# Weight rounding and norm scaling on ScalarE in a four-layer kernel: what moves, engine by engine

## What is computed

```
def _layernorm(x, axis=-1, eps=1e-05):
    m = jnp.mean(x, axis=axis, keepdims=True)
    v = jnp.var(x, axis=axis, keepdims=True)
    return (x - m) / jnp.sqrt(v + eps)
...
        # layer 1's attention: 16 heads of 8 features, 77 keys
        scores = jnp.einsum('bhqd,bhkd->bhqk', q, k) / math.sqrt(D_K)
        scores = jnp.where(m, min_value, scores)
        attn = jax.nn.softmax(scores, axis=-1)
        attn = jnp.where(m, 0.0, attn)
        x = jnp.einsum('bhqk,bhkd->bhqd', attn, v)
...
        # layer 2's feed-forward
        gate = fp4_linear(x, w_gate)
        y = fp4_linear(x, w_up)
        h = jax.nn.silu(gate) * y
        return fp4_linear(h, w_down)
...
        # layer 3's mixture; layers 0 and 1 have mixtures of 8 experts, top 2, of their own form
        h = jax.nn.relu(jnp.einsum('td,edh->eth', xf, w1) + b1[:, None, :])
        y = jnp.einsum('eth,ehd->etd', h, w2) + b2[:, None, :]
        out = jnp.einsum('etd,te->td', y, gf)
...
    x = x + jnp.tanh(g_xattn[0]) * _L0_xattn_ref(_layernorm(x, axis=-1), ctx_1024, ctx_1024, L0_xattn_Wu, L0_xattn_Wv)
    # and so on: one attention and one feed-forward part per layer, four layers
```

## Time and profile before

| quantity | value |
|---|---|
| median of 3 runs | 809.17 us (815.39, 809.17, 808.51) |
| profiled execution, its own time | 815.81 us |
| its span | 814.1 us |
| mean granted clock of TensorE | 0.886 |
| PE busy | 727.3 us (89%) |
| DVE busy | 546.1 us (67%) |
| ACT busy | 371.1 us (46%) |
| POOL busy | 208.1 us (26%) |

### The profile page before, as it was taken

The page is one execution under the profiler, slowest core; times in us unless marked ns, Lnnn a source line. Parts: engine busy times, 40 slices in busy tenths (PEclk is TensorE's granted clock), DMA queues, the critical chain, the costliest instruction groups (busy, mean ns, idle before and its releaser), DMA issues.

```text
span 814.1 us, 10005 instructions
## 1 busy us (share of the span) xinstructions
PE 727.3 (89%) x3459; PEld 572.7 (70%) x3459; DVE 546.1 (67%) x1226; ACT 371.1 (46%) x663; POOL 208.1 (26%) x193
## 2 busy tenths in 40 slices
PE   4989999999999798987999988994659999799997
PEld 2789977888966575865767766773446888577775
DVE  5686769544367767358575765597894554678996
ACT  3365444122235745636338374531213443386773
POOL 5141025320014123114342512035002320213532
PEclk9699999555589999999999989997688999789999
DMA  5120020100000200020202020011000000011000
GB/s 129 40 83 1 1 66 15 65 0 1 0 1 14 65 14 27 0 65 0 79 13 66 18 62 0 1 42 52 0 1 0 2 1 1 4 47 28 1 1 26
DMA packets 27362, 20.97 MB, mean 26 GB/s; under 512 B 5410, under 2 KB 22572, under 8 KB 27312
## 3 DMA queue, kind: packets, MB, share of 16 engines
q1 hardware_dynamic: 26591, 20.29, 8.4%
q10 hardware_dynamic: 720, 0.04, 0.1%
HBM read 19.80 MB, written 0.52 MB: 25 GB/s over the span
## 4 chain that ended last, share of the span: by engine, by line
PE 69%; DVE 18%; issue 4%; ACT 4%; POOL 3%; DMA 1%; ACTq 0%; DVEq 0%; POOLq 0%
PE PS L1433 60%; PE PS L1654 4%; DVE H2l L1124 2%; POOL WL L622 2%; PE PS L1539 2%; ACT H1h L796 1%; PE PS L1590 1%; DVE XN L951 1%; DVE SN L1079 1%; DVE WH L977 1%; PE PS L1454 1%; ACT G L794 1%; DMA GW<-in_L_gate_T 1%; POOL RSTD L632 1%; DVE H1l L1124 1%
## 5 line engine op out<-in xcount | busy, mean ns | idle before, releaser
L622 POOL TENSOR_TENSOR WL<-RAW,WH 128x512 fp32r<-128x512 f32 (+2 forms) x76 | 93.7, 1248 | 166.3 <-DVE WH L977 142.3
L1124 DVE TENSOR_TENSOR H2l<-G,H2h 128x512 fp32r<-128x512 f32 x104 | 84.0, 822 | 62.0 <-ACT H2h L796 61.0
L1124 DVE TENSOR_TENSOR H1l<-G,H1h 128x512 fp32r<-128x512 f32 x80 | 64.6, 814 | 29.5 <-ACT H1h L796 28.6
L1433 PEld LDWEIGHTS PS<-V,ATT 77*128 77x128 f32 x512 | 82.3, 243 | 1.0 <-issue 0.6
L1433 PE MATMUL PS<-V,ATT 77*128 77x9 f32 x512 | 78.7, 282 | 0.0
L813 ACT ACTIVATE ATT<-ATT 128x308 f32<-128x308 f32 x64 | 29.4, 459 | 103.0 <-DVE ATT L1225 102.7
L1217 DVE TENSOR_REDUCE MX<-PS 128x4 f32<-128x308 f32 x64 | 30.5, 477 | 66.9 <-PE PS L1433 66.9
L615 POOL TENSOR_TENSOR RSTD<-VE,MHALF 128x4 f32<-128x4 f32 x18 | 19.3, 1070 | 212.1 <-DVE VE L941 212.1
L1433 PE MATMUL PS<-H1h,WH 128*128 128x512 f32 x146 | 62.1, 425 | 8.0 <-DVE H1l L1124 8.0
L794 ACT ACTIVATE G<-PS,UB 128x512 f32<-128x512 f32 x64 | 44.8, 699 | 40.7 <-PE PS L1433 36.4
L1433 PE MATMUL PS<-XTh,WH 128*128 128x512 f32 x128 | 55.5, 434 | 8.5 <-POOL WL L622 5.3
(11 more groups left out here) (246 smaller groups left out, 1680.3 us busy)
## 6 DMA issues: line engine op xcount, KB each, us to landing
RAW<-in_L_ffn_spec_W SPq DMA_DIRECT2D x4, 1024.0 KB, 5.6
RAW<-in_L_ffn_w SPq DMA_DIRECT2D x16, 256.0 KB, 3.1
RAW<-in_L_ffn_up_W SPq DMA_DIRECT2D x8, 256.0 KB, 2.8
RAW<-in_L_ffn_down_W SPq DMA_DIRECT2D x8, 256.0 KB, 3.3
RAW<-in_L_ffn_spec1a_W SPq DMA_DIRECT2D x2, 512.0 KB, 4.0
RAW<-in_L_ffn_spec1b_W SPq DMA_DIRECT2D x2, 512.0 KB, 5.1
RAW<-in_L_ffn_wg SPq DMA_DIRECT2D x4, 176.0 KB, 2.7
RAW<-in_L_ffn_wu SPq DMA_DIRECT2D x4, 176.0 KB, 2.8
```

The lines of the kernel that those rows point to most:

```text
L622: g.tensor_tensor(lo, RAW[0:r["rows"], r["raw"] + s["c0"]:r["raw"] + s["c1"]], hi.bitcast(fp32), ALU.subtract).then_inc(lo_done, 1)
L1124: v.tensor_tensor(lo, full, hi.bitcast(fp32), ALU.subtract).then_inc(split_done, 1)
L1433: return t_.matmul(o, l, r, start=start, stop=stop)
```

## The change

- `scaled` moves from DVE to ACT everywhere, as `Identity(rstd · x + nmr)` (L734). For this POOL makes NMR = −mean · rstd behind each rstd (L618), DVE makes −mean (NM), and the third and later rstd wait for the scaling of the norm-step two before.
- `high_part` moves to ACT everywhere (L718): for layer 0's first strips, for the six strips of BEFORE[1] (groups 11 to 16 of layer 1's attention), for all strips of mixtures 1 and 3, and for the four strips of BEFORE[3], which leave layer 2 and stand in groups 2 to 5 of layer 3's attention.
- In layer 1 the bias rows are copied on ACT (groups 4, 5, 7 and 9) and subtracted on POOL (L688).
- The attention's weighting in layer 1 is done in PSUM: one `scalar_tensor_tensor` in place of a small scaling and a product into a buffer, then the sum into X.
- norm 4's first half ends in DVE's `stream_plus_norm(0)` at step 8 instead of 10.

The core of the diff:

```
@@ POOL rstd
-                    g.tensor_tensor(RSTD[:, c], VE[:, c], MHALF[:, c], ALU.pow).then_inc(rstd_ready, 1)
+                    if k >= 2:
+                        pool.wait_ge(xn_ready, TH * (k - 1))
+                    step(g.tensor_tensor(RSTD[:, c], VE[:, c], MHALF[:, c], ALU.pow))
+                    g.tensor_tensor(NMR[:, c], NM[:, c], RSTD[:, c], ALU.mult).then_inc(rstd_ready, 1)
@@ POOL, order
-            head_keys(1, CT, range(2, TH + 1))
+            head_keys(1, CT, range(2, 5))
+            for k in range(4):
+                pool.wait_ge(row_high, k + 1)
...
+                g.tensor_tensor(ROWr[32:33, c], ROW[32:33, c], ROWr[32:33, c].bitcast(fp32),
+                                ALU.subtract).then_inc(row_ready, 1)
+            pool.wait_ge(row_ready, 4)
             prepare(1)
...
-            rstd(10, 11)
-            prepare(3)
-            rstd(12, 13)
+            rstd(10, 11, 12, 13)
             pool.wait_ge(k3_ready, 2)
             head_keys(3, K3T, range(2))
             rstd(14, 15)
-            head_keys(3, K3T, range(2, B))
+            for b in range(2, B):
+                for s in BEFORE[3][3 * b - 6:3 * b - 3]:
+                    low_part(s)
+                head_keys(3, K3T, range(b, b + 1))
@@ ACT
+            def scaled(n, h, src, dst):
+                act.wait_ge(rstd_ready, NORM_STEP[n, h] + 1)
+                for t in range(TH * h, TH * h + TH):
+                    s.activation(dst[:, t, :], src[:, t, :], ACT.Identity, scale=RSTD[:, t:t + 1],
+                                 bias=NMR[:, t:t + 1]).then_inc(xn_ready, 1)
@@ ACT attention
+                    if first and 2 <= i < 2 + len(BEFORE[3]):
+                        high_part(BEFORE[3][i - 2])
+                    if not first and i == 6:
+                        scaled(2, 1, X, XN)
+                    if not first and i == TH * NG + WEIGH_LAG - 2 + 4:
+                        scaled(3, 0, X, XN)
+                    if not first and i == TH * NG + WEIGH_LAG - 2 + 9:
+                        scaled(4, 0, XN, XM)
+                    if not first and i in (4, 5, 7, 9):
+                        bias_row((4, 5, 7, 9).index(i))
...
+                    if not first and 11 <= i < 11 + len(BEFORE[1]):
+                        high_part(BEFORE[1][i - 11])
@@ DVE weighted, layer 1
-                        now(v.tensor_scalar(RC2[:, :], RC[:, :], ANY[:, t:t + 1], None, ALU.mult))
-                        rc = RC2
-                        dst = TMP
+                        now(v.scalar_tensor_tensor(o[:, :, 0:DK], o[:, :, 0:DK], ANY[:, t:t + 1], rc, ALU.mult, ALU.mult))
+                        y = X[:, t, :].rearrange("p (h d) -> p h d", h=NH)
+                        v.tensor_tensor(y, o[:, :, 0:DK], y, ALU.add).then_inc(o_done, 1)
@@ DVE, before layer 2's norm 6
-            norm(5, X, XN, summed(1))
-            prepare(3)
+            norm(5, X, summed(1))
```

More of the change, by code:

```diff
@@ L850, in gate @@
                 s.activation(RT[:, 1, :], RT[:, 0, :], ACT.Exp).then_inc(gate_exp, 1)
+            for h in range(2):
+                scaled(1, h, X, XN)
             turned(1, split=True)
@@ L875, in _ @@
             last.then_inc(wq_copied, 1)
+            for h in range(2):
+                scaled(5, h, X, XN)
             turned(4)
+            for h in range(2):
+                scaled(6, h, X, XN)
             turned(5, halves=(0,))
@@ L896, in _ @@
                     copy(HQT[0:I2 - 256, m + 2 * S:m + 3 * S], PS[4 + t % 2][0:I2 - 256, 2 * S:3 * S]).then_inc(f2_tc, 1)
+            for h in range(2):
+                scaled(7, h, X, XN)
             turned(6)
@@ L903, in _ @@
             heads_turned(1, PS[0])
+            for h in range(2):
+                scaled(8, h, X, XN)
             turned(7, split=True, halves=(0,))
@@ L959, in norm @@
                     stats(n, h, src)
-                for h in range(2):
-                    scaled(n, h, src, dst)
             def low_of_xt(n, halves=range(2)):
@@ L967, in low_of_xt @@
                     v.tensor_tensor(XTl[:, c], XT[:, c], XTh[:, c].bitcast(fp32), ALU.subtract).then_inc(xtl_ready, 1)
-            def high_part(s):
-                r = s["area"]
-                if s["strip"] == r["first"]:
-                    dve.wait_ge(loaded[r["n"]], 16 * len(area_loads(r)))
-                    if r["after_unit"] is not None:
-                        unit_used(dve, r["after_unit"])
-                hi, _ = weights(r, s["c0"], s["c1"])
-                v.tensor_copy(hi, RAW[0:r["rows"], r["raw"] + s["c0"]:r["raw"] + s["c1"]]).then_inc(hi_done, 1)
-            def prepare(layer):
-                for s in BEFORE[layer]:
-                    high_part(s)
             def per_token(m, row):
@@ L1263, in attention @@
                         weighted(g // NG)
-                        if layer == 1 and g // NG - first < 4:
-                            bias_row(g // NG - first)
                     if layer == 1:
```

91 lines of the change are left out of this document (41 added, 50 removed).

## The result

The changed kernel took 786.02 us in the median (781.40 to 787.82, four runs) against 809.83 for the kernel before, a ratio of 0.967 with an interval of 0.962 to 0.973: it is faster by 3.3%, where 823 us was forecast. The profiled execution took 787.46 us, with a span of 785.7 against 814.1, so 28.4 us are to be found between the two traces.

The account below looks back on a forecast made before the run. TensorE was taken to bound the kernel, with layer 1's attention at the lower clock the largest item. 809.2 + 2.5 (smaller terms and new waits) − 40 (layer 1) + 51 (layer 3) = 822.7, so 823 us; range 795 to 858.

Parts of the forecast that it names:

- −40: Layer 1's attention and tail: with work off VectorE the clock stays at 1.00, saving 33.4, 6.6 and 2.2 us, some 2 given back.
- 0.9 was forecast: Start of mixture 1: norm 3's second half stands between ScalarE's pairs, +0.9 us.
- the −7: Mixture 1: 34 high parts leave VectorE, and 7 of some 32 us of TensorE waits are gained (bounds 2 and 12).
- That group's step would be 3.0 us: Layer 3's attention, group 8: TensorE waits 1.0 us for GpSimd's head keys (bounds 0.3 and 2.0), and the clock falls.
- the term of +50: Layer 3's loop behind group 8: clock at 0.50 to the loop's end, 44 us, and the tail, 6.5.
- the price (+51): Layer 3's attention: 44 us for 23.5 groups at the lower clock, 6.5 for the tail, and the 1.0 us wait.
- All terms move alike: Whole kernel: terms read from the 815.81 us profiled execution were applied unchanged to the 809.2 us median.
- The wait at group 20: Layer 1's attention: TensorE waits about 0.6 us for GpSimd's head keys of batch 5 (bounds 0 and 1.5).
- Rival 2: Layers 1 and 3: both loops keep their clock, 772 us, if layer 3's wait is under about 0.5 us; chance 0.19.
- Mixture 3: 0: Mixture 3: TensorE is full and ScalarE, busy 43.56 of 60 us, gains twelve strips; no change in time.
- norm 5: Norm 5: ScalarE scales only after W2's five copies, so the first matmul on the turned result comes 2.6 us later.
- norm 6: Norm 6: its eight scale steps no longer wait beside GpSimd's head keys, −1.2 us (bounds −4 and +0.5).

## Layer 1's loop: what held the clock

The forecast gave this stage −40 and said that VectorE's relief does it. To see which relief, the moved pieces go back to VectorE: the scaling of norm 2's second half, the six high parts, and the bias rows, as the kernel before has them.

> The changed kernel with the three pieces of layer 1's attention on VectorE again: norm 2's second-half scaling, the six high parts and the bias rows (copies and subtractions). Theory A (VectorE's extra work made the steps that came before the clock's fall): the clock falls near group 14 as before and the loop costs 3.84 us per group, so about 786 + 35 = 821 us (815 to 828). Rival B (the fall came from something else that the change took away, such as the shorter weighting, or is a matter of chance): 786 to 792 us with a granted clock of 1.00.

Measured: 785.4 us (783.8 to 788.0), the rival's case. Nothing of the 35 us came back. One thing was left of the change in this loop: the weighting in PSUM, three operations behind the reciprocal made two. Undone as well:

```
-                        now(v.scalar_tensor_tensor(o[:, :, 0:DK], o[:, :, 0:DK], ANY[:, t:t + 1], rc, ALU.mult, ALU.mult))
+                        now(v.tensor_scalar(RC2[:, :], RC[:, :], ANY[:, t:t + 1], None, ALU.mult))
...
+                        step(v.tensor_tensor(X[:, t, :], X[:, t, :], TMP, ALU.add))
```

> As the run before last with layer 1's attention on VectorE (785 us, clock 1.00), and also the weighting as the kernel before had it (one small operation more per batch, 1.09 us instead of 1.00 until the next operation). In the traces the two kernels differ at group 11: before, GpSimd's head keys began 0.03 us ahead of VectorE's copy of turns, and the first high part behind it took 1.93 us; without the small operation VectorE's copy began 0.05 us ahead of the head keys, the high part took 0.41 and the head keys 3.08. Theory D (a collision decided by these 0.1 us set the late step of 2.45 us and the fall): with the old weighting the high part takes about 1.9 us again, the clock falls near group 14, 815 to 825 us. Rival (the clock in this loop is a matter of chance, or another part of the change holds it): 784 to 790 us.

816.0 us (814.2 to 818.4). And alone, in the kernel before:

> The kernel before with only the weighting of layer 1 done in PSUM, one small operation fewer per batch; all else (scaling, high parts, bias rows) stays on VectorE. Theory D (the 0.1 us decide which of the two engines goes first at group 11): granted clock 1.00 through layer 1's loop and 809 - 36 = 773 us (768 to 780), faster than the changed kernel. Rival (the moved work is what matters, the weighting gives 0.1 us per batch): 806 to 810 us with 0.50 from group 14.

775.5 us (771.0 to 775.9), ratio 0.959 with 0.954 to 0.965. **One saved operation of 0.23 us per batch is worth some 32 us, more than the whole change gives**; the rest of the change together costs 7 (by the ratios) to 10 us (by the medians). The rows show how. First place, group 11, DVE and POOL of the kernel with the weighting in PSUM and all else on VectorE:

```profile
141.81 0.41 DVE L1024 CAST WH<-RAW 128x512 fp32r<-128x512 f32 x1
...
142.92 1.72 DVE L1024 CAST WH<-RAW 128x512 fp32r<-128x512 f32 x1
...
141.27 3.08 POOL L663 TENSOR_TENSOR BDK<-CT,HM 128x1232 f32<-128x1232 f32 x1 [6.73 <-PE PS L1455]
```

and of the one with the old weighting, in which the DVE cast stands behind head keys that had begun at 140.35:

```profile
140.97 1.93 DVE L1026 CAST WH<-RAW 128x512 fp32r<-128x512 f32 x1
```

DVE's copy of turns ahead of the cast began 0.05 us before POOL's head keys in the first and 0.02 us after them in the second (at 141.22 and 140.37). In the first the head keys were stretched, from 2.27 to 3.08 us, and PE never waited; in the second the cast took 1.93 and the step after group 13 was 2.45 us, the very step that stood ahead of the fall in the earlier trace rows. But this kernel's clock did not fall there. It fell at the second place, group 20:

```profile
155.21 1.85 DVE L1273 TENSOR_SCALAR RC<-RC,ANY 128x16 f32<-128x16 f32 x1
...
158.07 2.44 DVE L1365 CAST ROWr<-ROW 1x512 fp32r<-1x512 f32 x1
...
154.77 2.25 POOL L665 TENSOR_TENSOR BDK<-CT,HM 128x1232 f32<-128x1232 f32 x1
...
162.40 1.36 PE L1461 MATMUL PS<-BDK,ATT 128*128 128x308 f32 x2 [3.26 <-DVE ATT L1258]
```

The small operation that the weighting in PSUM saves, 16 elements per partition and 0.235 us in the median, took 1.85 us beside the head keys of batch 5; the bias row's cast took 2.44 beside those of batch 6; peak and below of the next group came late and TensorE waited 3.26 us. The clock reads 1.00 up to 160.1 and 0.50 from there, 1.0 us into this wait (159.14 to 162.40).

Why the profiled execution of the kernel before fell at the first place already, on the same step of 2.45 us, stays open. Its usual execution probably fell at the second, too. That is an estimate, since no trace of one is kept: in the kernel of 810.0 us below, which has the same 2.45 and falls at group 20, layer 1's loop from group 14 to 31 is 7.0 us shorter than in the earlier trace rows, and 815.8 − 7.0 = 808.8 us is what the kernel before takes in the median (809.8).
 
With the weighting in PSUM the small operation isn't there (the new ones have an operand in PSUM and took 0.36 and 0.29), and the same place reads:

```profile
149.56 1.37 DVE L1328 CAST ROWr<-ROW 1x512 fp32r<-1x512 f32 x1
...
153.26 0.76 PE L1429 MATMUL PS<-BDK,ATT 128*128 128x308 f32 x2 [0.49 <-DVE ATT L1225]
```

The Trainium skill, page "SBUF — State Buffer", section "Who interferes with whom", tells of the lock between VectorE and GpSimd on a shared SBUF port. These rows agree: the operation of 16 elements, 1.85 us instead of 0.23, was held about as long as the cast of 512 (1.93).

**Is it the time or the place of the arithmetic?** The saved operation is issued again in front of the PSUM form, its result unused.

> The kernel before with the weighting in PSUM and the small operation that it saved issued again with its result unused, so that the arithmetic in PSUM stays and VectorE comes 0.27 us later at group 11 (1.27 us from reciprocal to bias row, 1.09 before, 1.00 in PSUM). Theory D (only the 0.1 us matter): the head keys start ahead of VectorE's copy, the first high part takes 1.9 us, a step of 2.4 us or more follows group 13 and the clock falls: 807 to 818 us. Rival E (the sum out of PSUM helps in some other way): 774 to 780.

810.0 us (805.7 to 816.4, ten executions). The first high part took 1.73, a step of 2.45 us followed group 13 without a fall, and the clock fell at group 20, within a wait of 3.36 us of TensorE for VectorE. Theory D's "only the 0.1 us" is half right: the fall came where the re-issued operation met the head keys (1.84 us at 149.94), not where the order of two starts was decided.

**Does the moved work also suffice?** The changed kernel with the old weighting:

> The changed kernel with the old weighting of layer 1 (product into a buffer, sum in SBUF), so that only the moved work is left of the change. Theory F (the moved work alone also keeps the clock: VectorE is at 41 of 66 us in the loop where it was full, and its high parts, which met the head keys, are gone): 785 to 789 us. Rival (without the saved operation the loop falls as before, whatever is moved): 815 to 825.

789.7 us in the median, one execution of four at 811.1. So yes, in three executions of four: the trace (789.1) keeps 1.00 through the loop, and the forecast's mechanism is sufficient there, it only wasn't the sole one.

**The bias rows.** In the kernel before they are moved to the tail of the loop, where VectorE is idle:

```
-                        if layer == 1 and g // NG - first < 4:
-                            bias_row(g // NG - first)
+                    if layer == 1 and i in (34, 35, 36, 38):
+                        bias_row((34, 35, 36, 38).index(i))
```

> The kernel before, with the four bias rows in steps 34, 35, 36 and 38 of layer 1's attention loop on VectorE, where it waits, instead of behind the first four batches' weighting; weighting, high parts and scaling as before (the sum into X waits for its end). Theory G (what decides is VectorE's SBUF-only work that meets the head keys: bias rows behind batches 1 and 2, the one saved weighting operation, the first high part; with the rows gone from groups 9 to 21 VectorE reaches the first high part earlier and the second meeting at group 18 loses its casts, leaving the small operation that took 1.84 us): the steps after group 13 stay at or under 2.3 us, clock 1.00, 775 to 780 us. Rival (the saved operation of the weighting is needed): a step of 2.4 us or more and a fall at group 14 or 20, 800 to 812 us.

781.9 us (780.5 to 783.8), with every step behind group 13 at 1.98 to 1.99 us. The time is 2 us above Theory G's range; in the tail the granted clock was 0.50 from 180 to 197. That is a third way to the same clock, with the old weighting, the high parts and the scaling all on VectorE. Three sufficient reliefs (a saved operation, moved work, moved bias rows) have in common only that less SBUF-only work of VectorE meets the head keys. VectorE's load itself is not the cause: this last kernel has the same load as the one before.

Layer 1's loop has a ladder, too, by the step ahead of group 20. With 5.3 to 5.5 us (three kernels, 18 executions) the time was that of a fall each time. With 2.44 to 2.63 us (eleven kernels, 40 executions) three executions, the falls of layer 3 aside, were 18 to 27 us above the highest of their kernel's others: 801.3, whose trace shows the fall, and 811.1 and 796.7, of which no trace is kept. So all that holds the clock here holds it most times, not always.

## The smaller terms, and a faster kernel

**Scaling.** The group of scale steps in the changed kernel; then ACT and PE at the start of mixture 1:

```profile
L734 ACT ACTIVATE XN<-X,NMR,RSTD 128x128 f32<-128x128 f32 x64 | 26.1, 483 | 23.1 <-POOL NMR L618 23.1
```

```profile
194.00 1.65 ACT L734 ACTIVATE XN<-X,NMR,RSTD 128x128 f32<-128x128 f32 x4 [0.89 <-POOL NMR L618]
...
197.57 0.50 PE L1440 MATMUL PS<-WH,H1h 128*128 128x512 f32 x1 [2.35 <-DVE H1l L1164]
...
199.70 0.79 PE L1440 MATMUL PS<-WH,H1h 128*128 128x512 f32 x1 [1.16 <-DVE H1l L1164]
```

A scale step takes 0.483 us in the mean on ScalarE (four of them 1.65) against 0.341 in the median on VectorE (four 1.11), and ScalarE stood idle 23.1 us for the product of GpSimd before them. At the start of mixture 1 ScalarE waits 0.89 us and scales for 1.65 before it comes to the hidden activations that TensorE waits for, 2.35 and 1.16 us. But the scale steps are the smaller part of the 4.7 us. The run with layer 1's pieces back on VectorE (785.4 us) has the same code here, with the same ScalarE scaling, and the stretch costs +1.4 in its trace. The windows of the changed kernel and of that one:

```profile
190.87:199.50 8.63, 5.31 (x19) 3.30 (x19) 4.55 (x23) 6.36 (x12) 2.05 (x3) 1.00 0.01 2
199.50:202.90 3.40, 3.20 (x7) 2.10 (x7) 1.58 (x4) 1.65 (x4) 1.39 (x2) 0.50 0.00 0
...
209.80:213.20 3.40, 3.40 (x10) 2.44 (x8) 0.00 (x0) 0.00 (x0) 0.00 (x0) 0.50 0.00 0
```

```profile
193.59:198.60 5.01, 5.01 (x12) 3.77 (x12) 1.95 (x11) 3.35 (x8) 1.21 (x2) 0.50 0.02 5
198.60:229.77 31.17, 28.45 (x121) 19.98 (x120) 18.31 (x45) 16.97 (x29) 10.21 (x12) 1.00 0.03 9
```

The changed kernel came into mixture 1 at 1.00, waited, and had two stretches at 0.50; the other came in at 0.50, as the kernel before does, doesn't show the wait of 2.35, and stayed at 1.00 after. All traces with this code and a start at 0.50 show +1.2 to +1.4, all that start at 1.00 show +4.7 or +4.8. So about 1.4 of the 4.7 us is the scaling (0.9 was forecast), and 3.3 come with the clock. The second stretch isn't even tied to ScalarE's scaling: the kernel of 768.7 us below, which scales on VectorE, has one at 0.50 from 201.0 to 204.4, for 1.8 us. Whether the waits behind the scale steps bring on the first isn't shown. In the same way projection and norm 8 cost 1.7 us in that run (3.1 in the changed kernel), and mixture 3 1.0 (2.6).

At norms 5 and 8 the steps stand on the chain:

```profile
515.38 3.19 ACT L734 ACTIVATE XN<-X,NMR,RSTD 128x128 f32<-128x128 f32 x8
```

```profile
670.78 0.76 PE L1440 MATMUL PS<-XTh,WH 128*128 128x512 f32 x1 [3.32 <-DVE XTl L1024]
```

The wait of 1.99 has become 3.32. These scale steps (norms 0, 1, 5, 7, 8 and the second halves of 3 and 4) back on VectorE:

> The changed kernel with the scale steps of norms 0, 1, 5, 7 and 8 and of the second halves of norms 3 and 4 back on VectorE (without the negated product on GpSimd for them); norm 2, the first halves of 3 and 4, norm 6 and all high parts stay on ScalarE. Theory (what the trace lost at norms 0 and 1, 5.2 us, at the start of mixture 1, 6.7, at norm 5, 3.0, and from norm 8 to the start of mixture 3, 5.7, comes from ScalarE's slower scaling, 1.65 us per four against 1.11, the added product and the place in its queue): 20.6 us at most, 16 expected, 770 us (766 to 775), if layer 1's and layer 3's loops keep their clock. Rival (those stretches lost by clock dips of their own): 780 to 786. A fall in one of the loops would give 805 to 820.

783.0 us in the median (774.9 to 801.3), 3 us under the changed kernel and in the rival's range; between the best executions it is 6.5 us (774.9 against 781.4), so of the 16 expected less than half came. The profiled one, 801.3, lost its clock behind group 20, where a wait of 0.31 us for head keys 5 and a step of 2.44 stand, as they do in the changed kernel, which kept it. Its trace shows why both are in part right. Against the kernel before, mixture 0's first matmul comes 0.6 us late there instead of 5.2, and norm 5 costs −0.1 instead of +2.8: these belong to the scaling. The start of mixture 1 costs 0.4, but it came in at 0.50, as in the runs that show 1.4; and projection and norm 8 cost 5.1, more than before the edit (3.1), with a granted clock of 0.72 from 658.6 to 685.1.

**Mixture 1's high parts** back on VectorE (`mixture` on each engine, layer 1 only):

> The changed kernel with the high parts of mixture 1's 34 strips on VectorE again; the loops and norms stay. Theory (mixture 1 gained 7.6 us from VectorE's relief): 786 + 7 = 793 us (790 to 796). Rival (the gain in mixture 1 is only clock dips that fall elsewhere after a shift of the whole): 784 to 788.

795.1 us (790.9 to 797.8), 9.1 more than the changed kernel, and mixture 1 from 260 to 539 costs −0.3 us in its trace instead of −7.6; the −7 is confirmed by a run.

**Together.** The weighting in PSUM and mixture 1's high parts on ScalarE, in the kernel before:

```
-                        elif kind == "split" and layer == 0:
+                        elif kind == "split" and layer < 3:
```

> The kernel before with the weighting in PSUM (775.5 us) and the high parts of mixture 1's 34 strips on ScalarE; everything else as before. Moving them back in the changed kernel cost 9.1 us (786.0 to 795.1), and the trace's own difference over mixture 1 was 7.6. Theory: the two gains add, 775.5 - 8 = 767.5 us (765 to 771). Rival (mixture 1's gain needs the other moves): 774 to 777.

**768.7 us in the median, ratio 0.952 with 0.946 to 0.958: the fastest kernel of this study**, faster than both. One of its four executions took 796.7, 28 us more, which is about what 15 groups at the lower level would cost, (3.84 − 1.985) × 15; its trace isn't kept.

Can it be made safe? The six high parts on ScalarE as well, a group earlier than the change has them:

> The kernel of the run with 768.7 us (weighting in PSUM, mixture 1's high parts on ScalarE) with the six high parts of layer 1's attention also on ScalarE, at groups 10 to 15, one group earlier than the changed kernel has them; norms and bias rows stay on VectorE. Theory (the loop's margin is set by VectorE and GpSimd meeting there; with the high parts on ScalarE neither the head keys of batch 4 nor those of batch 5 are late): no step above 2.4 us from group 13 on, clock 1.00 in every run, no outlier like the 796.7 us that one run of four showed, 766 to 770 us. Rival (ScalarE now has queries, turns and a high part in group 10 and is late, a step of 2.4 us there, and the clock falls in some run): 790 or more in at least one run.

801.6 us (801.4 to 802.1), each execution. The load left VectorE and the clock fell, every time. DVE, POOL and PE:

```profile
149.43 2.36 DVE L1331 CAST ROWr<-ROW 1x512 fp32r<-1x512 f32 x1
151.82 2.62 DVE L1332 TENSOR_TENSOR ROWr<-ROW,ROWr 1x512 fp32r<-1x512 f32 x1
...
149.07 4.82 POOL L655 TENSOR_TENSOR BDK<-CT,HM 128x1232 f32<-128x1232 f32 x2
...
155.60 1.37 PE L1431 MATMUL PS<-BDK,ATT 128*128 128x308 f32 x2 [3.15 <-DVE ATT L1227]
```

The low parts ended elsewhere, so two head-key steps stood back to back and the bias row of batch 2 met both. The same kernel with the rows in steps 34 to 38, and the kernel of 768.7 with the same edit:

> The kernel of 801.6 us (in it also the six high parts on ScalarE), whose bias row of batch 2 took 0.55 + 2.36 + 2.62 us on VectorE beside two head-key steps of 4.82 together and made a step of 5.29 us at group 20, with the bias rows in steps 34, 35, 36 and 38. Theory G: that step is near 2.0 to 2.3 us, clock 1.00, 766 us (764 to 769). Rival (the high parts on ScalarE at groups 10 to 15 are what costs): 795 or more.

> The kernel of 768.7 us (weighting in PSUM, mixture 1's high parts on ScalarE) with the bias rows in steps 34, 35, 36 and 38. Theory G: the step of 2.63 us at group 20 (a cast of a bias row that took 1.37 beside head keys) goes, no run falls, 767 us (765 to 769) without an outlier like 796.7. Rival: same as before, 768 and an outlier.

775.4 us for the first (771.6 to 776.3): 26 us back by moving four bias rows. 775.4 for the second (771.1 to 777.0): no outlier, but slower in the median, and neither has the 766 or 767 expected. A part of it is that in the tail the rows stand in front of the last weighting. PE's first matmul of mixture 1, there and in the kernel of 768.7:

```profile
186.19 0.77 PE L1431 MATMUL PS<-XTh,WH 128*128 128x512 f32 x1 [5.27 <-DVE XTl L969]
```

```profile
184.67 0.77 PE L1431 MATMUL PS<-XTh,WH 128*128 128x512 f32 x1 [1.44 <-DVE XTl L969]
```

At last the rows spread over steps 23, 28, 32 and 36:

> The kernel of 775.4 us whose bias rows stood in steps 34 to 38 and delayed mixture 1's first matmul (it waited 5.27 us there, 1.44 in the kernel of 768.7), with the rows in steps 23, 28, 32 and 36, clear of the head keys of batches 5 and 6 and with one in the tail. Theory G: no step over 2.3 us in groups 13 to 31, the wait before mixture 1 under 3 us, 766 us (763 to 769), no run above 775. Rival (a row in steps 23 to 32 makes a long step or a fall of its own): 780 to 800 in some runs.

775.6 us (766.9 to 776.7, six executions). All steps from group 13 are 1.985 us, as wanted, and the wait before mixture 1 is 1.02 us, but the tail is no shorter: from layer 1's first scores to the first matmul of mixture 1 it takes 76.1 us, against 75.0 with the rows in steps 34 to 38 and 71.9 in the kernel of 768.7. In place of the wait there is a granted clock of 0.62 between 174 and 192, in the tail. The execution of 766.9 us had the highest mean clock (0.942 against 0.924 to 0.931). What decides the clock in the tail stays open.

## Why the prediction was wrong, step by step

- **The step that failed** is "That group's step would be 3.0 us ... So I take it that the clock falls at group 8 or 9". The delay was right in sum, 0.94 us against 1.0, and right in its cause for group 8, but it was put in one group. It came in two, 0.5 at group 6 (ScalarE's first high part ahead of a copy, which my sum let hide) and 0.42 at group 8, whose step was 2.41 us; the clock stayed at 1.00, and the term of +50 measured 0. With group 8 late by 1.06 (and group 6 as before) the clock fell in one execution of two, with 1.68 in four of four: that a wait there takes the clock, and the price (+51), stand, and the size of the single wait was off by half. The bounds of that term, 0.3 to 2.0, held it; the rival that ends on the other side said "if layer 3's wait is under about 0.5 us", and that is what came. It had a chance of 0.19 and should have had more, since a bound of 0.3 lay inside my own estimate and the one fall on record stood behind a step of 2.93 and one of 2.45.
- **Layer 1** came out at −39.1 for −40, by a cause that was right as far as it went: the moved work does hold the clock (789.7 with the old weighting). What I wrote off in one clause, "a weighting with one short operation fewer per batch is small beside it", does it alone. I had added up busy times; the operation's 0.23 us is its time when nobody is beside it. The −40 was read from a trace that fell at group 14 and was taken off a median of executions that probably fell at group 20, so "All terms move alike" was wrong by some 5 us: the traces differ by 28.4, the medians by 23.8.
- **The wait at group 20**, 0.6, measured 0.31 of idle time (a step of 2.44, so 0.45 late).
- **Rival 2** (both stay, 772) is the case that came. It was 14 us too low. 5 of them are the difference between trace and median just named. The others are in the table: the start of mixture 1 3.8, norms 0 and 1 1.9, projection and norm 8 1.6 and mixture 3 2.6. The scale step was priced at 0.27 to 0.33 us with room for a short product, and it measured 0.39 from start to start, with the product and its waits in front; that is about the 1.9 of norms 0 and 1 (16 steps; the traces with this code show 5.2 to 7.8 us there). Of the other three, the run of 785.4 us has 0.5, 0.2 and 1.0 with the same code; the rest, 6.3 us, goes with stretches at 0.50 in the changed kernel's trace. The forecast had no term for such stretches outside the loops, and what decides them is open. "Mixture 3: 0" overlooked its own start, where a second half's copies now stand behind two high parts.
- **Mixture 1** (−7, measured −7.6, and 9.1 by the run), **norm 5** (+2.6, +2.8) and **norm 6** (−1.2, −0.8) were right.

## What to carry to other kernels

Where TensorE fills a loop and its clock has been seen to fall, cost a change by the steps it makes longer, not by the sum of busy times: delays of 0.5 and 0.4 us in two groups left the clock alone, 0.5 and 1.7 cost 50. Look for the small operations of VectorE that touch only SBUF and for the GpSimd operations beside them; keeping them apart, or giving them an operand in PSUM, was worth as much in layer 1's loop as moving VectorE's extra work, without that work's price elsewhere. Before you put a difference between two traces down to the edit, set the granted clock of the same stretch beside it: 3.3 of the 4.7 us at the start of mixture 1 were that. And measure such a kernel several times: one program gave 775 and 801 us.

## What I had not expected of the hardware

- An operation of 16 elements per partition took 1.85 us beside a GpSimd operation of 2.25 (0.235 in the median), a cast on a single partition 2.44.
- Which engine was held went with who began: with VectorE's copy 0.05 us ahead, head keys took 3.08 us and the cast 0.41; with it 0.02 us behind, 2.27 and 1.93.
- At the lower level (0.50) TensorE was busy 99.73 of 100 us, and the clock did not come back within the loop in any trace.
- The clock can fall within a wait, long before TensorE works again: it fell 1.0 us into a wait of 3.26, 1.2 into one of 1.53 and 2.1 into one of 2.29; behind the wait of 0.91 it fell 0.3 us after its end.
- A kernel with VectorE's high parts moved to ScalarE (801.6) was 33 us slower than the same with them on VectorE (768.7), through a bias row that neither edit touched.
